# Shared experts' down products from split operands, expert by expert, in a perceiver block kernel

## The reference, cut to what matters

```python
def _L0_ffn_ref(x, gate_w, gate_bias, w1, w3, w2, sw1, sw3, sw2):
    xt = x.reshape(-1, shape[-1])
    scores = jax.nn.softmax((xt @ gate_w.T).astype(jnp.float32), axis=-1)
    _, idx = jax.lax.top_k(scores + gate_bias, TOPK)
    weights = jnp.take_along_axis(scores, idx, axis=1).astype(x.dtype)
    y = jnp.zeros_like(xt)
    for e in range(N_EXPERTS):
        gate_e = jnp.sum(jnp.where(idx == e, weights, 0.0), axis=1)
        h = jax.nn.silu(xt @ w1[e].T) * (xt @ w3[e].T)
        y = y + gate_e[:, None] * (h @ w2[e].T)
    z = jax.nn.silu(xt @ sw1.T) * (xt @ sw3.T) @ sw2.T
    return (y + z).reshape(shape)
```

## Time and profile before

| what | us |
|---|---|
| median of 3 runs | 448.68 (448.63 to 451.23) |
| profiled execution, device time | 448.59 |
| its span in the profile | 446.8 |
| PE busy in the span | 429.9 (96%) |
| DVE busy in the span | 307.0 (69%) |
| ACT busy in the span | 175.5 (39%) |
| mean granted TensorE clock | 0.985 |

### The profile page before, as it was taken

How to read it: one execution, slowest core, us unless ns; L and a number is a source line. 1 busy time by engine, 2 the same in 40 slices (tenths; PEclk the granted TensorE clock), 3 DMA queues, 4 the chain that set the end, 5 groups by cost and what they waited for, 6 DMA issues and landing times.

```text
span 446.8 us, 8180 instructions
## 1 busy us (share of the span) xinstructions
PE 429.9 (96%) x3184; PEld 287.5 (64%) x3184; DVE 307.0 (69%) x572; ACT 175.5 (39%) x235; POOL 73.8 (17%) x78
## 2 busy tenths in 40 slices
PE   5998999999999999999999999999999999999996
PEld 2953345744445756688865398884457788888872
DVE  5541235698889899886658966510475899999965
ACT  1102111387752211022223243110337778888730
POOL 1000000000023700228631100155100000000061
PEclk9999999999998999999779999999999999999999
DMA  8999959836212530065000200044989999999545
GB/s 318 433 428 425 425 244 321 266 92 187 102 32 94 161 91 9 4 266 208 3 0 0 96 0 2 24 166 85 269 305 389 347 373 412 377 397 396 223 135 170
DMA packets 17937, 92.41 MB, mean 207 GB/s; under 512 B 3424, under 2 KB 5104, under 8 KB 10736
## 3 DMA queue, kind: packets, MB, share of 16 engines
q1 hardware_dynamic: 14880, 78.82, 47.4%
q10 hardware_dynamic: 1488, 8.93, 5.8%
q0 software_dynamic: 1536, 4.20, 2.9%
HBM read 82.25 MB, written 12.08 MB: 211 GB/s over the span
## 4 chain that ended last, share of the span: by engine, by line
PE 82%; DVE 9%; SPq 2%; DMA 2%; issue 1%; ACT 1%; POOL 1%; DVEq 0%; ACTq 0%
PE bank L921 34%; PE bank L735 8%; PE bank L660 6%; PE bank L686 4%; PE bank L569 3%; PE bank L523 3%; PE bank L547 3%; PE bank L590 3%; PE bank L499 2%; SPq L333 2%; DVE part L1496 2%; PE bank L711 2%; PE bank L897 2%; DVE x L1712 1%; PE bank L712 1%
## 5 line engine op out<-in xcount | busy, mean ns | idle before, releaser
L1496 DVE SCALAR_TENSOR_TENSOR part<-ring,cols,part 128x504 f32<-128x504 f32 (+13 forms) x64 | 42.0, 715 | 0.1
L735 PEld LDWEIGHTS bank<-ring 64*64 64x64 f32 x960 | 33.4, 140 | 10.2 <-issue 8.8
L735 PE MATMUL bank<-ring 64*64 64x64 f32 (+1 forms) x960 | 37.8, 230 | 0.8 <-issue 0.7
L686 PE MATMUL bank<-xnT,ring 128*128 128x512 f32 (+1 forms) x96 | 37.7, 544 | 0.7 <-ACT xnT L1080 0.7
L427 POOL TENSOR_TENSOR small<-small 128x1 f32<-128x1 f32 (+2 forms) x12 | 12.1, 1005 | 134.6 <-DVE small L1373 73.6
L660 PE MATMUL bank<-early,ring 128*32 128x512 f32 (+15 forms) x512 | 33.3, 402 | 0.3 <-DVE early L1515 0.3
L1496 DVE SCALAR_TENSOR_TENSOR ring<-bank,cols,ring 128x504 f32<-128x504 f32 (+2 forms) x36 | 26.3, 733 | 5.1 <-ACT ring L1128 4.1
L686 PEld LDWEIGHTS bank<-xnT,ring 128*128 128x128 f32 x96 | 17.6, 190 | 17.2 <-issue 14.5
L1262 ACT ACTIVATE rows<-bank 128x512 f32<-128x512 f32 x19 | 11.4, 598 | 39.5 <-PE bank L921 39.5
L660 PEld LDWEIGHTS bank<-early,ring 128*32 128x32 f32 x512 | 14.5, 112 | 15.2 <-issue 11.2
L436 POOL TENSOR_TENSOR ring<-ring,consts 128x256 f32<-128x256 f32 x20 | 15.8, 815 | 46.8 <-DVE ring L1628 32.5
(11 more groups left out here) (256 smaller groups left out, 903.5 us busy)
## 6 DMA issues: line engine op xcount, KB each, us to landing
early<-wffn_in SPq DMA_DIRECT2D x21, 1024.0 KB, 7.4
ring<-ctxT_in SPq DMA_DIRECT2D x4, 2048.0 KB, 26.3
ring<-ctx_in SPq DMA_DIRECT2D x4, 2048.0 KB, 30.7
raw1b<-wffn_in SPq DMA_DIRECT2D x6, 1024.0 KB, 9.8
raw3b<-wffn_in SPq DMA_DIRECT2D x6, 1024.0 KB, 8.9
raw2b<-wffn_in SPq DMA_DIRECT2D x6, 1024.0 KB, 7.9
ring<-firw_in SPq DMA_DIRECT2D x4, 1024.0 KB, 4.9
xs<-zeros_in ACTq DMA_DIRECT2D x1, 3840.0 KB, 13.9
```

Source lines behind the costliest of these rows:

```text
L686: last = pe.matmul(bank[QB[g % 3]][:, ts], wqkv[:, j, c, h * P:(h + 1) * P], xnT[:, c, ts], start=(c == 0), stop=(c == DC - 1))
L735: last = pe.matmul(dst[s, d], left[s, L * t:L * (t + 1)], right(s, t), start=True, stop=True)
L1496: return dve.scalar_tensor_tensor(out=d, in0=s, scalar=w, in1=d, op0=ALU.mult, op1=ALU.add)
```

## The change

1. `shared_down(e, t)` is one expert at a time: first all four tiles of expert 0, then all four of expert 1, in the same PSUM banks 4 to 7 (`first=(e == 0)`, `final=(e == NSH - 1)`). Each call has 12 fp32r matmuls in three terms in place of 4 plain f32 ones. It waits for the low part of the expert's w2 (`w_lo[2]`) and for the low parts of its four hidden tiles (`hT_lo`).
2. ACT gets `high_shared` for the two shared w2 pieces and `high_hidden` for the eight hidden tiles, between the silus. DVE gets `low_shared` and `low_hidden` for the same. The high w2 of expert 0 lies in `xgT`, that of expert 1 in a new tile `w2h1`; the high hidden tiles of both experts lie in the two halves of `w1a`; the low parts replace the raw values in place.
3. Since `w1a` is then in use, routed blocks take w1 and w3 from the other set (`pair_of`): block 0 loads to `raw1b`/`raw3b` and splits into `w1b`/`w3b`, block 1 loads to `early` and splits into `w1a`/`w3a`. The order of the loads stays. `yg`, where the last rows are gathered, moves to `early`.
4. DVE's list between the shared and the routed products changes: after the add of tile 0 comes the low part of w3 of block 1, and that of w1 of block 1 comes after the add of tile 3. ACT's high w1 of block 1 waits for the downs of expert 0 (`sd_first`).
5. Counts of `w_lo[2]` and `hT_lo` are offset accordingly; `iota` signals `ld_late` and `ld_iota` is gone.

```diff
-            def shared_down(t):
-                w = [use_raw(e, e) for e in range(NSH)]
-                pe.wait_ge(S["prod_ready"], NSH * FC)
+            def shared_down(e, t):
+                pe.wait_ge(w_lo[2], e + 1)
+                pe.wait_ge(S["hT_lo"], FC * (e + 1))
                 ts = slice(t * P, (t + 1) * P)
-                products(bank[4 + t][:, :], [(hTe[e][:, f, ts], w[e][:, f, :]) for e in range(NSH)
-                                             for f in range(FC)]).then_inc(S["sd_done"], 1)
+                hidden, w = (hTh[e], hTl[e]), (w2h[e], w2l[e])
+                last = products(bank[4 + t][:, :], [(hidden[hi][:, f, ts], w[wi][:, f, :]) for f in range(FC)
+                                                    for hi, wi in ((0, 0), (0, 1), (1, 0))],
+                                first=(e == 0), final=(e == NSH - 1))
...
+            for t in range(NT):
+                shared_down(0, t)
             for t in range(NT - 1):
-                shared_down(t)
+                shared_down(1, t)
             turn_rows(0, 0)
-            shared_down(NT - 1)
+            shared_down(1, NT - 1)
...
             for n in range(NSH * FC):
                 silu_of(n, 2 * (n % 2))
+                if n in (2, 3):
+                    high_shared(n - 2)
+                if n >= FC:
+                    high_hidden(2 * (n - FC))
+                    if n < NSH * FC - 1:
+                        high_hidden(2 * (n - FC) + 1)
...
+            high_hidden(NSH * FC - 1)
...
-                act.wait_ge(S[name], FC if isinstance(j, int) and j == 0 else NSH * FC + j - 1)
-                high(which, NSH + j, r)
+                if isinstance(j, int) and j == 1 and which == 0:
+                    act.wait_ge(sd_first, 1)
+                act.wait_ge(S[name], NSH * FC if isinstance(j, int) and j == 0 else NSH * FC + j - 1)
+                high(which, NSH + j, r, pair_of(which, r))
...
             for n in range(FC, 2 * FC):
                 shared_hidden(n)
+                low_hidden(2 * (n - FC))
+                low_hidden(2 * (n - FC) + 1)
+                if n < FC + NSH:
+                    low_shared(n - FC)
...
-                if t < 2:
-                    low_routed(1, 1, t)
+                if t == 0:
+                    low_routed(1, 1, 1)
...
                     rows_low(0, 0)
+            low_routed(1, 1, 0)
```

More of the change, by code:

```diff
@@ L91, in perceiver_block @@
         xnT = sb("xnT", [P, DC, NTOK])
+        w2l = [None, None]
+        with ExitStack() as over_early:
+            sb("over_up", [P, 2, 2048], held=over_early)
+            w2l[0] = sb("w2l0", [P, FC, D], F32R, held=over_early)
         early = sb("early", [P, 3, 2048])
@@ L110, in perceiver_block @@
         raw1[1] = sb("raw1b", [P, 2048])
+        hTl = [None, None]
+        with ExitStack() as over_shared:
+            w2l[1] = sb("w2l1", [P, FC, D], F32R, held=over_shared)
+            hTl[0] = sb("hTl0", [P, FC, 512], F32R, held=over_shared)
         raw2[1] = sb("raw2b", [P, 2048])
@@ L181, in perceiver_block @@
         hraw = hTe[0][:, 0:2, :]
+        hTh = [w1s[0][:, e, :].rearrange("p (f n) -> p f n", f=FC) for e in range(NSH)]
+        w2h = [xgT[:, :, :, :].rearrange("p i j n -> p (i j) n"), w2h1[:, :, :]]
         def yg(i):
-            return (raw1, raw3)[i // NT][1][:, 512 * (i % NT):512 * (i % NT + 1)]
+            return (raw1, raw3)[i // NT][0][:, 512 * (i % NT):512 * (i % NT + 1)]
         firw = [flat[:, FIRN * i:FIRN * (i + 1)].rearrange("p (g m n) -> p g m n", g=STK, m=FW) for i in (0, 1, 2, 0)]
@@ L273, in after, with pair_of, piece @@
             eng.wait_ge(s, signal(ins, s))
-        def piece(which, r):
-            return splits[which][r % 2][:, :, :].rearrange("p i (c n) -> p i c n", c=DC)
+        def pair_of(which, r):
+            return (r + 1) % 2 if which < 2 else r % 2
+        def piece(which, b):
+            return splits[which][b][:, :, :].rearrange("p i (c n) -> p i c n", c=DC)
         def loaded(n, r):
@@ L382, in load_up @@
                 for which in range(2):
-                    sp.wait_ge(w_lo[which], NSH + j - 1)
+                    sp.wait_ge(w_lo[which], NSH if isinstance(j, int) and j == 0 else NSH + j - 1)
                     load_piece(j, r, which, expert)
@@ L922, in products, with use_piece @@
                 return last
-            def use_piece(which, n, r):
+            def use_piece(which, n, b):
                 pe.wait_ge(w_lo[which], n + 1)
[L926 to L930, removed]
+                return piece(which, b)
             def shared_up(e, f, lo=0, hi=NT):
@@ L1020, in routed_down @@
             def routed_down(j, r, between=None):
-                pe.wait_ge(w_lo[2], j + 1)
-                w = piece(2, r)
-                pe.wait_ge(S["hT_lo"], j + 1)
+                w = use_piece(2, NSH + j, pair_of(2, r))
+                pe.wait_ge(S["hT_lo"], NSH * FC + j + 1)
                 if not isinstance(j, int) or j >= 2:
@@ L1189, in _, with high @@
                 act.activation(tm[:, h], bank[h][:, 0:NT * L], ACT.Copy).then_inc(S["t1_ready"], 1)
[L1190 to L1195, removed]
+            def high(which, n, r, b):
+                act.wait_ge(ld_raw[which][b], loaded(n, r))
+                raw = raws[which][b]
+                act.activation(splits[which][b][:, 0, :], raw[:, :] if b else raw, ACT.Copy).then_inc(w_hi[which], 1)
             def keep_solved(h, b):
@@ L1687, in _, with low @@
             mean_square(0, 2, 6)
-            def low(which, n, r):
+            def low(which, n, b):
                 dve.wait_ge(w_hi[which], n + 1)
-                split, raw = splits[which][r % 2], raws[which][r % 2]
-                dve.tensor_tensor(split[:, 1, :], raw[:, :] if r % 2 else raw, split[:, 0, :].bitcast(F32),
+                split, raw = splits[which][b], raws[which][b]
+                dve.tensor_tensor(split[:, 1, :], raw[:, :] if b else raw, split[:, 0, :].bitcast(F32),
                                   ALU.subtract).then_inc(w_lo[which], 1)
@@ L1852, in _, with low_shared, low_hidden @@
             dve.tensor_scalar(slot_g[:], rs_b[:, 0:TOPK * NT], zero_row, None, ALU.add).then_inc(S["gather_ready"], 1)
+            def low_shared(e):
+                dve.wait_ge(w_hi[2], e + 1)
+                dve.tensor_tensor(w2l[e][:, :, :].rearrange("p f n -> p (f n)"), raw2[e][:, :] if e else raw2[e],
+                                  w2h[e].rearrange("p f n -> p (f n)").bitcast(F32), ALU.subtract).then_inc(w_lo[2], 1)
+            def low_hidden(n):
+                dve.wait_ge(S["hT_hi"], n + 1)
+                dve.tensor_tensor(hTl[n // FC][:, n % FC, :], hTe[n // FC][:, n % FC, :],
+                                  hTh[n // FC][:, n % FC, :].bitcast(F32), ALU.subtract).then_inc(S["hT_lo"], 1)
             for n in range(FC, 2 * FC):
                 shared_hidden(n)
+                low_hidden(2 * (n - FC))
+                low_hidden(2 * (n - FC) + 1)
+                if n < FC + NSH:
+                    low_shared(n - FC)
             def low_routed(j, r, which):
-                low(which, NSH + j, r)
+                low(which, NSH + j, pair_of(which, r))
             def low_down(j, r):
-                dve.wait_ge(w_hi[2], j + 1)
+                dve.wait_ge(w_hi[2], NSH + j + 1)
                 split, raw = w2s[r % 2], raw2[r % 2]
```

51 lines of the change are left out of this document (34 added, 17 removed).

## The result

| what | before | after |
|---|---|---|
| median, us | 449.08 (20 runs) | 453.23 (20 runs) |
| ratio to before, 95% interval | | 1.0087 (1.0067 to 1.0107) |
| profiled execution, us | 448.59 | 453.04 |
| its span, us | 446.8 | 450.9 |
| mean granted clock | 0.985 | 0.973 |

What follows compares the result with a forecast made beforehand. It took PE as the bound, with a second chain from the fourth load's landing through DVE ending at the same moment. Sum: 448.59 + 0.2 + 1.7 = 450.5, stated as 450.6 us; range 448.2 to 453.9.

Steps and rivals of the forecast that it cites:

- The case with the largest chance: Around block 0's start: half clock for some 3.4 us, costing 1.7 us; chance 0.60.
- a long fall: PE's first products for blocks 0 and 1: 10.2 us at half clock, 5.1 lost, 454.0 us in all; chance 0.12.
- Shared downs: PE's shared downs: 21.8 us in place of 27.7, through at 327.1 in place of 333.6, 6.5 us earlier.
- Splits: New ACT copies (8.6 us) and DVE subtractions (10.0 us) while both wait for PE: costed at nothing.
- Landing unchanged: Fourth 1 MB load, raw w3 of block 1: lands about 327.1 as before, shift taken as 0.
- DVE's order, +0.6: DVE's list before block 0: one more add ahead of the rows, so block 0 starts at 334.2, 0.6 us later.
- w2 no longer late: Block 0's w2, asked for near 327.5: DVE's 0.33 us wait goes, block 0's down starts only 0.2 us later.
- The clock, +1.7: PE after its 7.1 us wait before block 0: half clock for a 3.4 us stretch after the restart, 1.7 us lost.
- the loop's period unchanged: Routed blocks after block 0: same matmuls and splits per block, so 0 us.
- the clock stays low for long: Rival, PE's first products for blocks 0 and 1: 10.2 us at half, 5.1 lost, 454.0 us; chance 0.12.
- The saving counts: Rival, start of block 0: fourth piece lands early enough, PE goes straight on, 442.2 us at best; chance 0.08.

Runs made afterwards that it cites:

- e2_swap: Changed kernel with DVE's low part of w3 of block 1 moved back behind the add of tile 1; one execution, 448.05 us, not to be compared by its time.
- e6_info: Changed kernel with GpSimd's scatter of the info table moved ahead, not waiting for the last shared up product; 447.50 us, ratio to before 0.9947.
- e3_rows: Changed kernel with the rows of block 0 split ahead of block 1's pieces; 450.72 us, ratio to before 0.9998.
- e1_warm: Changed kernel with eight plain products of constants on TensorE right after the last shared down; 449.71 us, ratio to before 0.9999.
- e4_load: Changed kernel without SyncE's wait for the eighth hidden product before the routed loads; 443.78 us, ratio to before 0.9867.

## Why the prediction was right or wrong

By the profiled executions 4.45 us were lost, where the sum said 1.9. The measured 453.2 is inside the range all the same: the range reached up to nearly the whole price of a long fall of the clock. The case with the largest chance (0.60, some 3.4 us at half clock) did not happen; a long fall, given 0.12, did, with part of it inside the wait. That the time fell inside is in part luck. The parts:

- *Shared downs*: right. 327.4 against 327.1.
- *Splits*: right, free, although DVE went to 11.24 us busy in 16.5.
- *Landing unchanged*: it came 0.7 later (22.9 against 22.2 after the product). Over the executions here it was between 20.6 and 22.9 with the scatter in its old place, so that is its spread and no effect of the change that I could show.
- *DVE's order, +0.6*: right, 0.61 by e2_swap. With the landing, block 0 starts 1.3 later.
- *w2 no longer late*: right. From the hidden product to block 0's down it is 6.43 us (344.10 to 350.53) against 6.86: 0.43 back, where the sum took back 0.42.
- *The clock, +1.7*: this is the step that failed, in size. It fell as forecast, with 10.2 us at half, the longer of the two stretches that I had, of which 4.1 lay in the wait. The sum took the shorter one. What it cost is in the starts of TensorE's groups: block 0's first group and the turn take 5.96 (334.92 to 340.88) against 3.24 before (333.60 in the earlier trace rows to 336.84), and the next group 0.1 more, 2.8 in all in place of 1.7. The reason given for the short stretch, dense products after the wait, did not hold: 6.2 us of them ran at half clock. The Trainium skill's rule, "TensorE: Matmul & The Clock Gate" (Part 1), that an idle TensorE falls back to half rate and is given the full one only for sustained work, agrees: here the clock fell 3.5 us into the wait and was full again only after 6.2 us of products. That rule does not account for the fall at 218.9 in the earlier trace rows, before which TensorE is recorded as busy all the time.
- *Left out*: two small terms, taken at nothing ("the loop's period unchanged"). From the turn of block 3's rows (352.52 before, 356.24 after) to the last turn (425.57, 429.70) it takes 73.46 us after and 73.05 before, +0.4: every second group of 36 products takes about 8.35 us, where three of those four took 8.20. And outside the span it is 2.14 us against 1.79 (+0.35), about the same in all versions with the split downs. Why was not tried for either.

So 1.3 + 2.8 - 0.4 = 3.7 to block 0's down, and 3.7 + 0.4 + 0.35 = 4.45. Of the rivals, "the clock stays low for long" was the nearest by its mechanism, and its 5.1 us too much because it counted the part inside the wait (half of 4.1, 2.0 us). "The saving counts" did not happen, and its reason is refuted: the loads are as slow beside split downs as beside plain ones (45 GB/s from 308 to 310 in both).

## What to carry to other kernels

When one engine is the whole chain, find the second chain that ends at the same join, and subtract it before costing a saving. Here a saving of 6 us could be had only if the split of one piece came 7.5 us sooner, and it was there in full once the two loads ahead of that piece were issued when their address was known, rather than when another engine was done. And time taken from TensorE ahead of a wait was worse than nothing here: it turned work into emptiness, none of the saving was left, and the half clock behind the wait cost 2.8 us on top. Where the wait stayed, products of constants in it won the loss back, and no more. Where the clock falls at other places of the program too, two versions can be told apart to 1 us only with the mean granted clock of their executions beside the times.

## What the runs showed of the hardware

- The granted clock fell even for a wait of 2.75 us (e6_info), and then only after TensorE was back at work. Windows of that execution (columns as in the earlier trace rows):

```profile
330.00:332.00 2.00, 0.00 (x0) 0.00 (x0) 2.00 (x5) 0.00 (x0) 0.00 (x0) 1.00 1.03 348
332.00:334.00 2.00, 1.87 (x7) 1.59 (x8) 2.00 (x3) 0.00 (x0) 0.00 (x0) 0.85 1.02 406
334.00:336.00 2.00, 2.00 (x6) 1.52 (x6) 0.82 (x1) 0.00 (x0) 0.00 (x0) 0.50 1.01 426
336.00:338.00 2.00, 2.00 (x11) 1.64 (x10) 0.18 (x1) 1.41 (x3) 0.00 (x0) 0.80 0.95 360
```

  It is full in the wait, half from about 333.4 to 336.8, and full again. So the price of a gap can fall due after it is over, while the stretch of the gap itself shows a clock of 1.00. That the gap made the clock fall is inferred: it fell in or behind each of the four waits of 2.75 to 7.51 us here (changed kernel, e2_swap, e3_rows, e6_info), and not at this place where TensorE was kept busy (e1_warm, e4_load).
- 1024 writes of 8 bytes from GpSimd's scatter in the stretch of four 1 MB loads go with a landing 2.5 to 4.8 us later (e6_info), where the bytes are 8 KB against 4 MB. Beside two such loads (e4_load) they did not make it slow: 5.3 us from issue to landing, against 17.5.
